# Weight loads through GpSimd's queue into eight slots, rounding by a clip of the low 16 bits, down weights over 40 slabs

## The reference

```python
xn = layernorm(x)                                   # over the last axis
g, v, d = xn @ Wg + bg, xn @ Wv + bv, xn @ Wd + bd  # 1024 x 1024 each
h_t = (0.001 + 0.998 * sigmoid(d_t)) * h_{t-1} + sigmoid(g_t) * tanh(v_t)

wq(w) = clip(round(w / m), -1, 1) * m,  m = max(mean(|w|), 1e-5)
aq(y) = round(y * 127 / a) * a / 127,   a = max(max|y| of the token, 1e-5)
gate, up = silu(aq(xn) @ wq(w_gate).T), aq(xn) @ wq(w_up).T     # 1024 -> 4096
out = x + h + aq(gate * up) @ wq(w_down).T                      # 4096 -> 1024
```

## Time and profile before

| | |
|---|---|
| median of 3 runs | 1830.42 us (1826.57 to 2071.62) |
| the profiled execution's own time | 1822.38 us |
| its span on core 5, the slowest | 1820.8 us |
| spans of the other cores | 1794.8 to 1816.9 us |
| mean granted clock of TensorE, by core | 0.968 to 0.984 |
| PE, DVE, ACT, POOL busy | 93%, 56%, 39%, 1% |
| DMA queue q1 (HWDGE) | 264.29 MB, 57.6% of 16 engines |
| DMA queue q0 (software, GpSimd) | 2.11 MB, 0.7% |

### The profile page before, as it was taken

The page is one execution under the profiler, slowest core; times in us unless marked ns, Lnnn a source line. Parts: engine busy times, 40 slices in busy tenths (PEclk is TensorE's granted clock), DMA queues, the critical chain, the costliest instruction groups (busy, mean ns, idle before and its releaser), DMA issues.

```text
span 1820.8 us, 22873 instructions; the slowest of 8 cores (1794.8 to 1820.8 us)
## 1 busy us (share of the span) xinstructions
PE 1692.8 (93%) x7686; PEld 756.4 (42%) x7686; DVE 1011.1 (56%) x1615; ACT 712.3 (39%) x830; POOL 10.8 (1%) x20
## 2 busy tenths in 40 slices
PE   2798879878988899999999999999999999999999
PEld 1343334333433344444444444444444444444434
DVE  3655548898569754455454554554645554455432
ACT  2567767577767522122222232222322223222210
POOL 0000000000000000000000000000000000000000
PEclk9999999999999999999999999999999999999999
DMA  7899999888999733533353336435432534462242
GB/s 204 245 272 317 309 310 292 254 259 262 323 244 273 120 88 91 76 93 87 76 82 76 81 94 101 85 76 76 104 76 75 82 78 92 90 100 66 62 99 98
DMA packets 267554, 267.94 MB, mean 147 GB/s; under 512 B 210480, under 2 KB 210608, under 8 KB 255152
## 3 DMA queue, kind: packets, MB, share of 16 engines
q1 hardware_dynamic: 266112, 264.29, 57.6%
q0 software_dynamic: 896, 2.11, 0.7%
q10 hardware_dynamic: 432, 0.08, 0.0%
HBM read 182.53 MB, written 33.57 MB: 119 GB/s over the span
## 4 chain that ended last, share of the span: by engine, by line
PE 70%; DMA 9%; DVE 9%; issue 5%; SPq 3%; ACT 3%; DVEq 0%; ACTq 0%
PE pb L644 44%; PE pb L595 24%; PE pb L447 3%; DMA wqst<-wup 2%; DMA wqst<-wgate 2%; SPq L203 2%; DVE hx L469 2%; DMA wast<-wattn 1%; DMA wdst<-wdown 1%; DMA xnT<-tr 1%; DVE sg L467 1%; DVE bn L222 1%; DVE bn L223 1%; DMA xin<-x 1%; SPq L216 1%
## 5 line engine op out<-in xcount | busy, mean ns | idle before, releaser
L644 PE MATMUL pb<-Wgq,xqT 128*128 128x512 fp8e4 x2048 | 487.1, 381 | 19.7 <-ACT H L670 10.9
L644 PE MATMUL pb<-Wuq,xqT 128*128 128x512 fp8e4 x2048 | 485.7, 380 | 3.1 <-DVE H L675 2.9
L595 PE MATMUL pb<-qT,Wdq 128*128 128x512 bf16 x2048 | 453.6, 380 | 4.0 <-DMA qT<-tr 4.0
L447 PE MATMUL pb<-xnT,Wa 128*128 128x512 bf16 x1536 | 355.6, 395 | 89.7 <-DMA xnT<-tr 43.4
L670 ACT ACTIVATE H<-pb,dx 128x512 f32<-128x512 f32 x256 | 173.0, 682 | 510.2 <-PE pb L644 425.0
L675 DVE SCALAR_TENSOR_TENSOR H<-pb,dx,H 128x512 f32<-128x512 f32 x256 | 191.2, 749 | 284.4 <-PE pb L644 223.9
L644 PEld LDWEIGHTS pb<-Wgq,xqT 128*128 128x128 bf16 x2048 | 200.2, 98 | 265.6 <-issue 28.4
L595 PEld LDWEIGHTS pb<-qT,Wdq 128*128 128x128 fp8e4 x2048 | 200.9, 98 | 247.7 <-issue 7.7
L644 PEld LDWEIGHTS pb<-Wuq,xqT 128*128 128x128 bf16 x2048 | 200.6, 98 | 247.9 <-issue 9.2
L447 PEld LDWEIGHTS pb<-xnT,Wa 128*128 128x128 bf16 x1536 | 154.0, 101 | 290.1 <-issue 125.7
L539 ACT ACTIVATE H<-H,cst,q_s 128x1024 f32<-128x1024 f32 x128 | 154.3, 1230 | 131.8 <-DVE dpall L534 131.8
(11 more groups left out here) (62 smaller groups left out, 665.9 us busy)
## 6 DMA issues: line engine op xcount, KB each, us to landing
xin<-x SPq DMA_DIRECT2D x64, 512.0 KB, 8.6
wqst<-wgate SPq DMA_DIRECT2D x32, 1024.0 KB, 10.8
wqst<-wup SPq DMA_DIRECT2D x32, 1024.0 KB, 10.6
scr_hT<-hx SPq DMA_DIRECT2D x64, 256.0 KB, 7.7
wqst<-wdown SPq DMA_DIRECT2D x16, 1024.0 KB, 8.8
hx<-scr_hT SPq DMA_DIRECT2D x64, 256.0 KB, 2.6
hx<-xT SPq DMA_DIRECT2D x64, 256.0 KB, 3.0
wdst<-wdown SPq DMA_DIRECT2D x16, 1024.0 KB, 6.6
```

The source lines that it names most:

```text
L447: return e.matmul(o, l, r, start=(k == 0), stop=(k == 7))
L595: return e.matmul(o, l, r, start=(c == 0), stop=(c == 31))
L644: return e.matmul(o, l, r, start=(k == 0), stop=(k == 7))
```

## The change

Weight loads (`load_wa` and `load_visit`) are issued from GpSimd's list. Its first instruction waits for the second x tile. Twelve slots of 8 KB per partition take the place of the two sets of four: four in Wdq's place (0 to 3), four in Wuq's place (4 to 7), and four in the upper part of D0 (8 to 11), of which up to eight serve the loads of gate and up. A slot's load is put in the list as soon as no unfinished visit of an earlier entry uses it. A `plan` lists all 96 visits with their slot; 16 of them have no load, because the slab stayed in its slot from its first pass (gate 10 to 15, up 0 to 3, down 0 to 5). The first pass of a slab to be kept writes its absolute values to `junk`, not over the slab. The order of passes is interleaved: gate first pass, 2 of up, 14 of gate second, 14 of up first, 2 of gate second, 16 of up second. 64 visits come at 64/56 per step from s = 7.

The second pass is now a multiplication with addition of MAGIC, by VectorE (two of three positions for gate and up, one of three for down) or by ScalarE, and one VectorE clip to -1 and 1 of the low 16 bits of each value, read as int16 with a step of two, into fp8. The visits of down are spread over slabs 0 to 19 and 22 to 39. The attention banks turn over seven, `late` is 1, the input tile's scales take fewer small operations and are split into `ffn_x1` and `ffn_dx`, and `quant_scales` has four operations where it had six. `group`, `silu`, `hidden` and `quant` hold the code of the slab loop in the same order as before, and `next_bank` gives the same turn over six banks shifted by one.

The core of the diff:

```diff
+        slot_at = [C0 + j * 8192 for j in range(4)] + [B0 + j * 8192 for j in range(4)]
+        slot_at += [D0 + 32768 + j * 8192 for j in range(4)]
+        slot32 = [at(f"slot{j}", [128, 2048], F32, a) for j, a in enumerate(slot_at)]
+        low16 = [t[:].bitcast(I16).rearrange("p (n two) -> p n two", two=2)[:, :, 0] for t in slot32]
+        junk = [at("junk0", [128, 2048], FP8, xqT_off), at("junk1", [128, 2048], FP8, bc_off)]
...
-            wa_full[t] = sp.dma(WL[t % 8], lambda e, o=wa_stage[t % 8], i_=d_wa[t]:
+            wa_full[t] = pool.dma(WL[t % 8], lambda e, o=wa_stage[t % 8], i_=d_wa[t]:
...
-        visits = [(0, 0, u) for u in range(16)] + [(1, 0, u) for u in range(16)]
-        visits += [(0, 1, u) for u in range(16)] + [(1, 1, u) for u in range(16)]
-        visits += [(2, 0, u) for u in range(16)]
-        n_c = len(visits)
-        visits += [(2, 1, u) for u in range(16)]
+        plan = []
+        def put(mat, second, u, slot, load=True, keep=False):
+            plan.append((mat, second, u, slot, load, keep))
+        for u in range(16):
+            put(0, 0, u, (u + 4) % 8, keep=u >= 10)
+        put(1, 0, 4, 4)
+        put(1, 0, 5, 5)
+        for u in range(10, 16):
+            put(0, 1, u, (u + 4) % 8, load=False)
+        for u in range(8):
+            put(0, 1, u, (u + 4) % 8)
+        for u in range(6, 16):
+            put(1, 0, u, u % 8)
+        for u in range(4):
+            put(1, 0, u, u, keep=True)
+        for u in range(8, 10):
+            put(0, 1, u, (u + 4) % 8)
+        for u in range(16):
+            put(1, 1, u, u % 4, load=u >= 4)
+        for k, u in enumerate(range(6, 16)):
+            put(2, 0, u, (0, 1, 2, 3, 8, 9, 10, 11, 0, 1)[k])
+        for u in range(6):
+            put(2, 0, u, (2, 3, 8, 9, 10, 11)[u], keep=True)
+        for u in range(6):
+            put(2, 1, u, (2, 3, 8, 9, 10, 11)[u], load=False)
+        for u in range(6, 16):
+            put(2, 1, u, 8 + (u - 2) % 4)
+        n_p1 = [max(v for v, p in enumerate(plan) if p[0] == mat and not p[1]) + 1 for mat in range(3)]
         v_full = {}
         v_done = {}
+        slot_free = {}
         sc_done = {}
         wq_done = {0: {}, 1: {}, 2: {}}
         abs_done = {}
-        def stage_of(v):
-            return (wq_stage[v % 4], wq_stage16[v % 4], UL[v % 4]) if v < n_c else \
-                (wd_stage[v % 4], wd_stage16[v % 4], DL[v % 4])
-        def load_visit(v, *toks):
-            mat, _, u = visits[v]
-            buf, _, s = stage_of(v)
-            free = v_done.get(v - 4) if v != n_c and (v < n_c or v >= n_c + 4) else None
-            v_full[v] = sp.dma(s, lambda e: e.dma_start(out=buf[:], in_=d_w[mat][u]), free, *toks)
+        junk_done = [None, None]
+        nv = {"load": 0, "done": 0}
+        def load_visit(v):
+            mat, _, u, slot, _, _ = plan[v]
+            v_full[slot] = pool.dma(UL[slot], lambda e: e.dma_start(out=slot32[slot][:], in_=d_w[mat][u]),
+                                    *slot_free.get(slot, ()))
+        def loads(last):
+            while nv["load"] < min(last, len(plan)):
+                v = nv["load"]
+                if plan[v][4]:
+                    if any(plan[w][3] == plan[v][3] for w in range(nv["done"], v)):
+                        return
+                    load_visit(v)
+                nv["load"] += 1
...
         def visit(v):
-            mat, second, u = visits[v]
-            buf, half, _ = stage_of(v)
+            mat, second, u, slot, load, keep = plan[v]
+            buf = slot32[slot]
+            full = [v_full[slot]] + ([] if load else slot_free[slot])
             c = 8 * mat
             if not second:
-                tok = act.do(lambda e, a=acc[:, mat * 16 + u:mat * 16 + u + 1]:
-                             e.activation(buf[:], buf[:], AF.Abs, bias=0.0, scale=1.0, accum_out=a), v_full[v])
-                v_done[v] = tok
+                col = acc[:, mat * 16 + u:mat * 16 + u + 1]
+                if keep:
+                    out = junk[mat // 2][:]
+                    tok = act.do(lambda e: e.activation(out, buf[:], AF.Abs, bias=0.0, scale=1.0, accum_out=col,
+                                                        saturate=False),
+                                 *full, last_scan["t"] if mat == 2 else None, junk_done[mat // 2])
+                    junk_done[mat // 2] = tok
+                else:
+                    tok = act.do(lambda e: e.activation(buf[:], buf[:], AF.Abs, bias=0.0, scale=1.0, accum_out=col),
+                                 *full)
+                slot_free[slot] = [tok]
                 abs_done[mat] = tok
                 return
             dst = Wq[mat][:, u * 2048:(u + 1) * 2048]
-            if u % 2 == 0:
-                tok = dve.do(lambda e, s=wsc[:, c + 3:c + 4]:
-                             e.tensor_scalar(dst, buf[:], s, None, OP.is_lt, saturate=False),
-                             v_full[v], sc_done[mat])
-                tok = dve.do(lambda e, s=wsc[:, c + 2:c + 3]:
-                             e.scalar_tensor_tensor(dst, buf[:], s, dst, OP.is_gt, OP.subtract, saturate=False), tok)
+            over = slot_free[u // 4 + (0 if mat == 2 else 4)] if mat else ()
+            s = wsc[:, c:c + 1]
+            if v % 3 == 0 or (mat < 2 and v % 3 == 1):
+                tok = dve.do(lambda e: e.tensor_scalar(buf[:], buf[:], s, MAGIC, OP.mult, OP.add), *full, sc_done[mat])
             else:
-                tok = act.do(lambda e, s=wsc[:, c:c + 1]:
-                             e.activation(buf[:], buf[:], AF.Identity, bias=C_MAGIC, scale=s),
-                             v_full[v], sc_done[mat])
-                tok = act.do(lambda e: e.activation(half[:], buf[:], AF.Relu, bias=C_NMAGIC1, scale=1.0), tok)
-                tok = dve.do(lambda e: e.tensor_scalar(dst, half[:], 2.0, -1.0, OP.min, OP.add, saturate=False), tok)
-            v_done[v] = tok
+                tok = act.do(lambda e: e.activation(buf[:], buf[:], AF.Identity, bias=C_MAGIC, scale=s),
+                             *full, sc_done[mat])
+            tok = dve.do(lambda e: e.tensor_scalar(dst, low16[slot], 1.0, -1.0, OP.min, OP.max, saturate=False),
+                         tok, *over)
+            slot_free[slot] = [tok]
             wq_done[mat][u] = tok
+        def visits_to(n):
+            while nv["done"] < n:
+                mat, second = plan[nv["done"]][:2]
+                if second and mat not in sc_done:
+                    return
+                loads(nv["done"] + 1)
+                visit(nv["done"])
+                nv["done"] += 1
...
+            t = dve.do(lambda e: e.tensor_reduce(q_s[:, 0:1], x[:], AX.X, OP.max, apply_absolute_value=True), t)
+            xq_max[i] = dve.do(lambda e: e.tensor_scalar(q_s[:, 1:2], q_s[:, 0:1], EPS, 1.0 / 127.0, OP.max, OP.mult), t)
+            ts = dve.do(lambda e: e.reciprocal(q_s[:, 2:3], q_s[:, 1:2]), xq_max[i])
+            xq_round[i] = act.do(lambda e: e.activation(x[:], x[:], AF.Identity, bias=C_MAGIC, scale=q_s[:, 2:3]), ts)
+        def ffn_dx(i):
+            j = 2 * (i % 2)
+            dve.do(lambda e, o=dx[:, j:j + 1], w=wsc[:, 1:2]: e.tensor_scalar(o, q_s[:, 1:2], w, None, OP.mult),
+                   xq_max[i], sc_done[0], silu_done.get(i - 2))
+            xq_scale[i] = dve.do(lambda e, o=dx[:, j + 1:j + 2], w=wsc[:, 9:10]:
+                                 e.tensor_scalar(o, q_s[:, 1:2], w, None, OP.mult), sc_done[1])
...
+            free = junk_done[0] if i == 0 else last_scan["t"] if i == 1 else xqT_free[i - 2]
+            xq_full[i] = turn(fill, xqT[j][:], free)
...
+        pool.need([x_full[1]])
         load_wa_to(8)
...
-                base = 3 * (s % 2)
+                bk = [(3 * s + mat) % 7 for mat in range(3)]
...
-                n, late = b + 1, 3 if b == 0 else 0
+                n, late = b + 1, 1 if b == 0 else 0
...
-                if s == 7:
-                    loads_to(4)
-                if s >= 8:
-                    visits_to((s - 7) * 64 // 54)
+                if s == 5:
+                    for j in range(4):
+                        slot_free[j] = [wa_free[16 + 2 * j], wa_free[17 + 2 * j]]
                 for mat in (0, 1):
-                    if mat in abs_done and mat not in mean_tok and nv["done"] >= 16 * (mat + 1):
-                        mean_tok[mat] = [s, mean_sum(mat), None]
+                    if mat not in mean_tok and nv["done"] >= n_p1[mat]:
+                        mean_tok[mat] = [s, mean_sum(mat)]
                     if mat in mean_tok and mat not in sc_done and s == mean_tok[mat][0] + 1:
                         mean_scales(mat, mean_bcast(mat, mean_tok[mat][1]))
+                if s >= 5:
+                    loads(n_p1[1] + 16)
+                if s >= 7:
+                    visits_to((s - 6) * 64 // 56)
+                if s == 57:
+                    ffn_x1(0)
                 if s == 58:
-                    ffn_x1(0)
-                if s == 59:
                     ffn_x2(0)
```

(26 more changed lines are left out.)

194 lines of the change are left out of this document (76 added, 118 removed).

## The result

The changed kernel is slower: 1878.97 us, median of runs from 1875.45 to 1891.21, against 1832.29 us for the kernel before in the same comparison. The ratio is 1.028 (95% interval 1.021 to 1.034). I had predicted 1752 us with a range of 1708 to 1802, so the time lies 127 us above the forecast and outside the range, on the other side of the kernel before.

What follows compares the result with a forecast made beforehand. It took transfers to bind the first half of the attention steps, VectorE's weight rounding the second half and 545 to 622 us. Terms -47, -17, -10 and -2 gave -76 from 1828: 1752 us, range 1708 to 1802.

Steps and rivals of the forecast that it cites:

- Queue: Weight loads on GpSimd's queue: issues of 0.55 to 0.77 us costed at nothing; transposes gain, no longer behind weights.
- Bytes: Steps 8 to 63: 91.9 MB in place of 102.4, 288 us with some moved ahead; transfers just stop binding.
- Steps 8 to 63: Attention steps after block 0: 314 us in place of 360.9, as 154 and 160 for the halves; -47 us.
- Feed-forward, slabs 0 to 45: Slabs before the first down group: less VectorE work cuts the loss from 28.8 to about 12 us; -17.
- Block 0: First eight attention steps: 10.3 us wait and about 4 for Wa go, less 4 for early statistics; -10.
- Start: Time before the first matmul: -2 us, range 0 to -4.
- Later slabs: Feed-forward after slab 45: no change, 0 us.
- C: Rival, VectorE's second-pass rounding: clip at one element per cycle, 1824 us, no change; chance 0.07.
- D: Rival, weight-load issue: GpSimd starved by VectorE, 1798 us at 5 us per load, about 1921 at 7; chance 0.07.
- A: Rival, steps, feed-forward and block 0: transfers still bind, -36 us, 1792 us; chance 0.18.
- B: Rival, whole kernel: TensorE becomes the bound everywhere, -109 us, about 1719 us; chance 0.08.

Runs made afterwards that it cites:

- e1: The changed kernel with attention and feed-forward weight loads put back in SyncE's list, all else kept: 1838.16 us, 1.008 of the kernel before.
- e2: The kernel before with only its weight loads moved to GpSimd's queue: 1946.52 us, 1.076 of the kernel before.
- e9: The kernel before with the new rounding alone; loads, queue and order stay: 1817.97 us, 0.996 of the kernel before.
- e5: As e1, with loads put in the list at most four visits ahead in place of eight: 1858.69 us, 1.019 of the kernel before.
- e11: As e1, with the down visits back on slabs 0 to 15 and 20 to 35: 1836.64 us, 1.007 of the kernel before.
- e10: The kernel before with 88 of its 96 slab loads bringing only half their columns, 46 MB less: 0.993 of the kernel before.
- m1: Separate test without the reference's computation: pairs of 256 KB transposes or plain stores, alone or with 1 MiB loads queued; transposes land in 3.2 us alone.

## Why the prediction was wrong

Point by point, against the profiled execution of the changed kernel:

- *"Queue ... I cost them at nothing ... The other bound is a gain: transposes no longer stand behind megabytes of weights."* This is the step that failed. I priced the queue at its issues, 0.55 to 0.77 us each, which was right, and looked for rivals only on the issuer's side. I didn't ask what a transpose in SyncE's queue would meet on the shared DMA engines. Rows 9 had the hint: the slow ones of the kernel before took 4.1 us to issue at a DMA share of 0.99, and the longest landing up to 700 us was 12.2 us. A transpose is some 1024 packets, and each of them lets an 8 KB packet of the other queue pass (648 against 646 from 308 to 323 us). In the place of "a gain" came 92.5 us of waits for xnT (43.4 before) and 29.0 for xqT (6.8 before); in the time the queue costs about 2% by e1, 7.6% by e2. The Trainium skill has the sentence that speaks against the hope, in "DMA: Bandwidth & Descriptors", section "Issuing engines are not separate DMA queues": several issuers save only the time of issuing. The trace agrees that nothing is gained, but shows a loss that the sentence doesn't tell of.
- *Bytes, "91.9 MB ... transfers stop being the bound, just".* The bytes are right: the page of after has 251.15 MB in all where before had 267.94, which is 16 slabs. The averaging over the whole stage was wrong: what matters is when slots come free, and the new plan has windows at DMA 0.07 to 0.72 and saturated ones between them (e1). By e1 against e9 (1.008 and 0.996) the plan and what came with it cost about 1.2% where I had counted a gain. I haven't divided this among the kept slabs, the early statistics and the moved scale operations; e5 and e11 exclude the lead and the down spread alone.
- *Steps 8 to 63, -47 us.* Measured: from the end of block 0 at 106.7 (103.24 and the last 16 matmuls of 0.216) to 473.5, 366.8 us, where before took 360.9, so +6. The size was wrong even without the queue: e10 and e9 show that taking away a third of the bytes in this stage, or the rounding's work, gives 0.4 to 0.7% each, 7 to 13 us (at best 23 for the bytes). I had let each half of the stage fall to its next floor at once (154 and 160 us). e10 runs 732 matmuls in its first two windows, where 833 would fit in the 180 us, and in its third VectorE is at 91%.
- *Feed-forward, slabs 0 to 45, -17 us.* Measured: 679.0 - 473.5 = 205.5 us for 158.8 of matmuls, 46.7 lost for 28.8, so +18; 23.33 of it is the one wait at 524.60 for xqT. In e1, 655.5 - 453.0 = 202.5. The spread gave nothing (e11).
- *Block 0, -10.* Measured 106.7 - 34.3 = 72.4 us for 62.2, so +10: the wait at its end is now 19.99 us, through VectorE's wait for `tr`. In e1 block 0 ends near 93.4 (91.65 and 8 matmuls), 1 us before the old 94.33: there the wait for xnT is gone and waits for Wa have taken its place.
- *Start, -2.* 34.30 for 32.11, so +2.

- *Later slabs, 0.* Measured +19: the last down block waits 9.21 us for 4.03, and at block boundaries there are six short stalls of 11.5 us together that the kernel before and e1 don't have, such as this one:

```profile
1159.98 1.89 PE L581 MATMUL pb<-Wgq,xqT 128*128 128x512 fp8e4 x8 [2.59 <-ACT H L591]
```

  ScalarE had just scaled the next block's x tile late, since VectorE had stood 16.94 us before that for the landing of a transposed qT. The weight loads are over by then, so I can't put this down to the queue by its traffic; what sets the core back here stays open.

Together 2 + 10 + 6 + 18 + 19 = 55 against a forecast of -76; the spans differ by 55.0.

Of the rivals, C (clip at one element per cycle) and D (GpSimd starved by VectorE) fell: 1227 ns and 551 to 594 ns. D was my only way to "slower", and it looked at the wrong resource. It cited the Trainium skill, "SBUF — State Buffer", section "SBUF: two separate sides"; that trap didn't show in the 104 loads of the changed kernel, whose groups took 551 to 594 ns each in the mean; which of VectorE's operations hold both port pairs no row shows. A (transfers still bind) was half right: they bind in bunches. B fell with the forecast.

What else stays open: why the DMA engines move only about 150 GB/s in some of the stalls; and what of the 1.2% belongs to which part of the plan.

## What to carry to other kernels

Before moving loads to another queue, list the small transfers on the critical path that stay behind, and ask how many bytes can be in flight beside them. Count their packets, not their bytes: while both queues have work, each packet of the small transfer lets one of the large one pass. In one in-order queue the place in the list bounds what a transfer waits for; in two queues its place bounds nothing, and a load issued later can still pass. Before counting bytes over a stage, follow the slots: kept data takes buffers from the rotation, and idle DMA windows beside full ones mean that the average will not be reached. And price a single remedy by the next bound in the same stage: here half of the slabs' bytes were worth 0.7%, the new rounding 0.4%.

## What was new of the hardware

- While two queues have work, the DMA engines give both the same number of packets: 452 and 453, 1545 and 1547, 216 and 211 in m1, 648 and 646 in the changed kernel. A transpose's packets are of 0.26 KB, those of a load in 8 KB rows of 8 KB, those of a load in 2 KB rows of 4.1 KB.
- A DMA transpose of 256 KB lands in 3.2 us alone and 22.4 us beside eight slabs of 1 MiB in another queue, software or hardware (22.0); a plain store of the same size in 2.3 and 11.1 us.
- The issue of a transpose can hold SyncE for 18 us (m1) to 24 us (after), so everything else on that list is late too.
- Smaller rows in the competing load (2 KB for 8 KB) changed little: the transpose's landing was 20.8 us in the median (13.8 to 25.0), the kernel's time 1.032 of before.
- A clip that reads every other int16 of 128x2048 and writes fp8 takes 1227 ns, the pace of a dense bf16 source.
- In the stall of 27 us before 328.48 TensorE's granted clock falls to 0.50, the 1.2 GHz level (310 to 330 us), and is at 0.83 from 330 to 340 us, where TensorE is busy throughout and runs 40 matmuls; from 340 to 350 us, at 1.00, it runs 48. So a stall costs more than its length.
